# One of eight weight blocks of each expert is multiplied whole, in fp32

## The chip, the core and the metric

The kernel runs on one core of a Trainium2 chip. The metric is the device time in microseconds, the median of several runs. TensorE multiplies, VectorE and ScalarE work on rows of 128 partitions, GpSimd and SyncE mostly issue DMAs. A core has 16 DMA engines that share the transfers of all queues.

## What is computed

A graph layer on 384 tokens of 1024 features, in fp32: a normalisation, a graph attention with 16 heads, a linear attention block with a small feed-forward part, the sum of these with the input, a second normalisation, and last a mixture of eight experts. Only the experts are touched by the change:

```python
logits = t @ switch_w + switch_b
route_prob = softmax(logits)
routes = argmax(route_prob)
for e in range(8):
    h = gelu(t @ w1[e] + b1[e])      # w1[e]: 1024 x 512
    y = h @ w2[e] + b2[e]            # w2[e]: 512 x 1024
    out = where(routes == e, y, out)
out = out * max(route_prob)
```

## The kernel before

**Precision.** A product in fp32 is made of fp32r products. Each weight block (128 partitions x 1024, 512 KB) is copied by ScalarE to fp32r, its high part (L763 for the experts, L591 before them), and VectorE subtracts that from the raw block and gets the low part (L912, called from `prep_x`, L1218). In the expert stage the tokens' high and low parts stand side by side in one stationary operand (64 tokens each), so a block is multiplied by four fp32r products of 128 x 512: two halves, high and low part of the weights. The rows of the two token parts are added afterwards.

**The blocks.** An expert has eight blocks: four of w1 (up) and four of w2 (down). They come in the order up(0), up(1), down(0), up(2), down(1) and so on to up(7), down(6), down(7), and are numbered by q; from Q_WO on block q lies in ring slot (q - Q_WO) mod 8. Slots 0 to 3 are `raw` with splits in `wsp`, slots 4 to 7 `raw_x` with splits in two buffers named `big`. So the down blocks of the first seven experts lie in slots 0 to 3, the up blocks in 4 to 7, and the last expert's down blocks in 4 to 7.

**Loads.** SyncE (SP) issues all loads in order of q. Before load q it waits until VectorE has split block q - 8 (`w_lo`, L402). Behind the preloaded ring this is a loop with registers over experts (L409).

**TensorE.** Before the stage it gathers the tokens of each expert, beside the first up product. Then for e = 0 to 6: up(e+1) with L1788 and the bias L1796, down(e) with L1827 and the bias L1833, hidden(e+1) with L1811, which turns and folds the up result of fp32 by four fp32 products of 64 columns. Then down(7). A product waits for the splits of its block (`open_quarter`). down(e) waits for `ht_lo`, the low part of its hidden values.

**ScalarE**, for each e: three copies of blocks, the copy of the up result (L826), three copies, the low rows of y (L844), gelu (L834), the hidden values' high part (L836), two copies. The last block copied ahead of L844 is the second down block of expert e+1.

**VectorE**, for each e: six splits, the sum of y (L1414), the hidden values' low part (L912, tile `big<-work,big`), two splits.

**GpSimd** writes y of each expert to memory (L562, 256 KB), and after the last one gathers the rows of y per token (L573). VectorE adds them (L1478), and SyncE writes the output.

Of the kernel before, what the change touches and what calls it, by code (L numbers as in the profile page):

```python
# [20 lines left out]
F32 = mybir.dt.float32  # L21
# [51 lines left out]

WO_ORDER = ((0, 0), (0, 1), (0, 2), (0, 3), (1, 0), (1, 1), (1, 2), (1, 3))

class Tally:
# [36 lines left out]
def graph_layer(nc, x, rowb, cols, consts, later, src_rows, dst_rows, src_cols, dst_cols, type_cols,  # L115
                type_weights, w_stream, w_experts, switch_w, b12, out):
    with ExitStack() as ctx:
# [3 lines left out]
        def sem(name):  # L121
            return ctx.enter_context(nc.semaphore(name))
# [119 lines left out]
        piece_done, codes_done = sem("piece_done"), sem("codes_done")  # L242
        raw_in = [sem(f"raw_in{n}") for n in range(XRING)]
        w_hi, w_lo = sem("w_hi"), sem("w_lo")
        w_started = sem("w_started")
        acc_ready, acc_hi, acc_free = sem("acc_ready"), sem("acc_hi"), sem("acc_free")
        elu_parts, elu_hi = sem("elu_parts"), sem("elu_hi")
        elu_lo = sem("elu_lo")
# [43 lines left out]
        def raw_slot(k):  # L292

            if k < RING:
                return raw[:, k, :]
            return raw_x[:, k - RING, :]
# [48 lines left out]
        @block.sync  # L345
        def _(sp):
            for t in range(NT):
                sp.dma_start(tok[:, t, :], x[t * P:(t + 1) * P, :]).then_inc(x_in[t], 16)
            sp.dma_start(cst[:], consts).then_inc(const_in, 16)
            sp.dma_start(bias[:], cols).then_inc(const_in, 16)  # L350

            def load(row, slot, split):

                if split is not None:
                    sp.wait_ge(w_lo, split)
                sp.dma_start(raw[:, slot, :], w_stream[bass.ds(row, P), :]).then_inc(raw_in[slot], 16)

            def load_piece(first, buf, read):

                for k, r in enumerate((src_rows, dst_rows)):  # L360
                    if read is not None:
                        sp.wait_ge(codes_done, read)
                    sp.dma_start(edge_rows[buf][:, k, :],
                                 r[bass.ds(first, N)].partition_broadcast(P)).then_inc(piece_in[buf], 16)

            for q in range(RING):
                load(q * P, q, None)
            for j in range(2):
                load_piece(j * N, j, None)  # L370
            with sp.Fori(0, (Q_MV - RING) // RING) as i:
                for j in range(RING):
                    row = sp.snap(i * (RING * P) + (RING + j) * P)
                    load(row, j, i * RING + (j + 1))
                    if j % 2 == 0:
                        first = sp.snap(i * (2 * N) + (2 + j // 2) * N)
                        load_piece(first, j // 2, i * 2 + (j // 2 + 1))
            for q in range(Q_MV, Q_GQ + RING):
                load(q * P, q % RING, q - RING + 1)
                if q % 2 == 0 or q >= Q_GQ:  # L380
                    n = (q - Q_MV) // 2 + 8 if q < Q_GQ else q - Q_GQ + 12
                    load_piece(n * N, n % 2, n - 1)
            assert n == PIECES - 1
            with sp.Fori(0, (Q_PAIR0 - Q_GQ) // RING - 1) as i:
                for j in range(RING):
                    row = sp.snap(i * (RING * P) + (Q_GQ + RING + j) * P)
                    load(row, j, i * RING + (Q_GQ + j + 1))
            for q in range(Q_PAIR0, Q_PAIR):
                load(q * P, slot_of(q), q - RING + 1)
            with sp.Fori(0, PAIRS - 1) as i:  # L390
                for j in range(3):
                    row = sp.snap(i * (3 * P) + (Q_PAIR + j) * P)
                    load(row, 1 + j, i * 3 + (Q_PAIR + j - 2))
            for q in range(Q_WO, Q_WO + RING):
                load(q * P, slot_of(q), q - RING + 1)
            sp.wait_ge(w_started, Q_WO - 1)
            for q in range(Q_WO + RING, Q_MOE):
                sp.dma_start(raw_slot(slot_of(q)), w_stream[q * P:(q + 1) * P, :]).then_inc(raw_in[slot_of(q)], 16)

            def load_expert(row, k, split):  # L400

                sp.wait_ge(w_lo, split)  # L402
                sp.dma_start(raw_slot(k), w_experts[bass.ds(row, P), :]).then_inc(raw_in[k], 16)

            for j in range(RING):
                load_expert(j * P, j, Q_MOE + j - XRING + 1)

            with sp.Fori(0, EXPERTS - 1) as i:  # L409
                for k in range(XRING):  # L410
                    first = QE + k if k < RING else k
                    row = sp.snap(i * (QE * P) + first * P)
                    load_expert(row, (RING + k) % XRING, i * XRING + (Q_MOE + RING + k - XRING + 1))
            q = Q_MOE + QE * EXPERTS - RING
            for j in range(RING):
                k = slot_of(q + j)
                load_expert(((EXPERTS - 1) * QE + RING + j) * P, k, q + j - XRING + 1)

            sp.wait_ge(route_done, 1)  # L420
            over = sp.value_load(rowi[0:1, OVER:OVER + 1], min_val=0, max_val=OVER)
            with sp.If(over > 0):
                q += RING
                for o in range(OVER):
                    r = sp.value_load(rowi[0:1, o:o + 1], min_val=0, max_val=(EXPERTS - 1) * QE * P)
                    for j in range(QE):
                        row = sp.snap(r + j * P)
                        load_expert(row, slot_of(q), q - XRING + 1)
                        q += 1

            for t in range(NT):
                sp.wait_ge(sum_done, t + 1)
                sp.dma_start(out[t * P:(t + 1) * P, :], tok[:, t, :]).then_inc(out_done, 16)
            sp.wait_ge(out_done, 16 * NT)
# [144 lines left out]
        def _(act):  # L579
# [178 lines left out]
            def prep_x(started=None):  # L758

                slot = slot_of(q_no.n)  # L760
                act.wait_ge(raw_in[slot], used[slot].add(16))
                act.wait_ge(w_started, q_no.value - (XRING - 2) if started is None else started)
                nc.scalar.activation(split_of(slot, 0), raw_slot(slot), ACT.Copy).then_inc(w_hi, 1)  # L763
                q_no.add()
# [135 lines left out]
        def _(dve):  # L900
# [316 lines left out]

            def prep_x():  # L1218
                slot = slot_of(q_no.n)
                dve.wait_ge(w_hi, q_no.add())  # L1220
                lo(split_of(slot, 1), raw_slot(slot), split_of(slot, 0)).then_inc(w_lo, 1)

            def projected(h, t):
# [259 lines left out]
        def _(pe):  # L1483
# [295 lines left out]

            u_no, ht_no, y_no = Tally(), Tally(), Tally()  # L1780

            def up_block(s, e, base, j):

                open_quarter()
                for kk in range(2):
                    k = 2 * j + kk
                    for a in range(2):
                        ins = nc.tensor.matmul(ps[:, e % 2, :], slot_x(k, s),  # L1788
                                               split_of(base + j, a)[:, kk * HALF:(kk + 1) * HALF],
                                               start=(k == 0 and a == 0), stop=False)  # L1790
                        if kk == 0 and a == 0:
                            ins.then_inc(w_started, 1)
# [22 lines left out]
            def down(s, e, base):  # L1815

                pe.wait_ge(ht_lo, ht_no.add())
                if y_no.n > 1:
                    pe.wait_ge(y_sum, y_no.n - 1)
                y_no.add()  # L1820
                for j in range(4):
                    open_quarter()
                    bank = 4 + 2 * (e % 2) + j // 2
                    for kk in range(2):
                        k = 2 * (j % 2) + kk
                        for a in range(2):
                            ins = nc.tensor.matmul(ps[:, bank, :], htk[:, e % 2, k, :],  # L1827
                                                   split_of(base + j, a)[:, kk * HALF:(kk + 1) * HALF],
                                                   start=(k == 0 and a == 0), stop=False)
                            if kk == 0 and a == 0:  # L1830
                                ins.then_inc(w_started, 1)
                    if j % 2:
                        ins = nc.tensor.matmul(ps[:, bank, :], slot_hot(s),  # L1833
                                               b12r[:, F + (j // 2) * HALF:F + (j // 2 + 1) * HALF],
                                               start=False, stop=True)
                        if j == 1 and s == EXPERTS - 1:
                            ins.then_inc(y_half, 1)
                ins.then_inc(y_ready, 1)
# [119 lines left out]
```

## Time and profile before

| | |
|---|---|
| median of 3 runs | 637.99 us (637.88 to 639.61) |
| profiled execution | 641.52 us |
| its span, first to last instruction | 639.8 us, mean granted clock 0.964 |
| TensorE matmul, weight load | 569.8 us (89%), 519.7 us (81%) |
| VectorE | 458.3 us (72%) |
| ScalarE | 318.3 us (50%) |
| GpSimd | 177.2 us (28%) |
| DMA | 102.69 MB, mean 161 GB/s |

The shares are means over the whole span. The expert stage begins near 521 us with the gathers and ends with the last output near 640 us. From 540 to 622 us the experts' products run, and the experts' weights (64 blocks, 32 MB) come mostly in this time.

### The profile page before, as it was taken

What the parts mean: (1) busy time and instruction counts of PE and PEld (TensorE: products, weight loads), DVE (VectorE), ACT (ScalarE), POOL (GpSimd) and SP (SyncE); (2) the same over time, 40 slices, a digit from 0 to 9 for tenths busy, and PEclk for the clock granted to TensorE, in tenths of its full rate; (3) what the DMA queues carried; (4) which work ended last, traced back from release to release, by engine and by line L of the source; (5) the groups of instructions that cost most, each with busy time, mean ns of one, the idle gap of its engine ahead of it and who ended that gap; (6) DMA issues with size and microseconds to landing.
All of it is one profiled execution on the core that took longest, in us unless ns stands there. A gap on an engine that the chain in (4) does not pass through costs nothing.

```text
span 639.8 us, 9211 instructions
## 1 busy us (share of the span) xinstructions
PE 569.8 (89%) x3090; PEld 519.7 (81%) x3090; DVE 458.3 (72%) x807; ACT 318.3 (50%) x475; POOL 177.2 (28%) x167
## 2 busy tenths in 40 slices
PE   3699999999999999999999998999898769888970
PEld 2699997888999999999889888899786657766750
DVE  6678887885455444735679899787879655999972
ACT  3445553320333333534366655675653345998960
POOL 5556765856399000710001022100001100000001
PEclk9889999999999999999999999999899959999986
DMA  8356558450533433395322443422662212999936
GB/s 298 134 189 181 171 155 245 115 130 1 183 120 129 164 125 122 107 277 141 96 81 83 105 98 99 105 98 69 228 198 84 80 34 89 330 413 411 412 109 211
DMA packets 33043, 102.69 MB, mean 161 GB/s; under 512 B 5392, under 2 KB 9552, under 8 KB 33008
## 3 DMA queue, kind: packets, MB, share of 16 engines
q1 hardware_dynamic: 27792, 90.02, 41.8%
q0 software_dynamic: 4912, 11.46, 6.8%
q10 hardware_dynamic: 304, 0.79, 0.4%
q8 instruction: 18, 0.29, 0.2%
q14 instruction: 17, 0.14, 0.1%
HBM read 96.65 MB, written 5.60 MB: 160 GB/s over the span
## 4 chain that ended last, share of the span: by engine, by line
PE 53%; DVE 27%; ACT 8%; DMA 6%; issue 5%; POOL 1%; DVEq 0%; ACTq 0%; SPq 0%; POOLq 0%
PE ps L1506 31%; DVE wsp L912 7%; DVE big L912 4%; PE ps L1520 4%; DMA raw<-in_w_experts 3%; PE ps L1685 3%; PE ps L1576 2%; ACT work L712 2%; PE ps L1639 2%; PE ps L1775 2%; PE ps L1614 2%; ACT wsp L591 2%; DVE work L984 2%; DVE pt L912 2%; PE ps L1827 1%
## 5 line engine op out<-in xcount | busy, mean ns | idle before, releaser
L1506 PE MATMUL ps<-big,wsp 128*128 128x384 f32 x1680 | 304.2, 339 | 9.2 <-DVE wsp L912 6.6
L1506 PEld LDWEIGHTS ps<-big,wsp 128*128 128x128 f32 x1680 | 294.4, 190 | 14.0 <-DVE wsp L912 6.4
L912 DVE TENSOR_TENSOR wsp<-raw,wsp 128x1024 fp32r<-128x1024 f32 x117 | 149.9, 1292 | 29.4 <-ACT wsp L591 23.3
L591 ACT ACTIVATE wsp<-raw 128x1024 fp32r<-128x1024 f32 x83 | 87.2, 1053 | 33.5 <-PE ps L1520 12.9
L509 POOL DMA_INDIRECT edge_table<-ef,eidx x48 | 57.4, 1195 | 31.9 <-DMA edge_table<-ef,eidx 19.1
L465 POOL TENSOR_SCALAR rs<-mv 128x1 f32<-128x1 f32 x12 | 9.3, 779 | 199.5 <-DVE mv L1232 102.3
L598 ACT ACTIVATE big<-ps,bias 128x384 f32 x24 | 14.0, 583 | 83.0 <-PE ps L1506 83.0
L923 DVE SCALAR_TENSOR_TENSOR big<-ps,bias,big 128x384 f32 x24 | 14.8, 618 | 51.7 <-ACT big L598 49.7
L912 DVE TENSOR_TENSOR big<-raw_x,big 128x1024 fp32r<-128x1024 f32 x36 | 42.0, 1214 | 0.3 <-ACT big L763 0.3
L763 ACT ACTIVATE wsp<-raw 128x1024 fp32r<-128x1024 f32 x34 | 34.5, 1049 | 7.0 <-DMA raw<-in_w_experts 4.3
L1827 PE MATMUL ps<-wsp,big 128*128 128x512 f32 x112 | 28.8, 399 | 9.6 <-DVE big L912 9.6
L763 ACT ACTIVATE big<-raw_x 128x1024 fp32r<-128x1024 f32 x36 | 36.0, 1046 | 0.1
L712 ACT ACTIVATE work<-work,snm 128x384 f32<-128x384 f32 x48 | 28.9, 604 | 12.7 <-DVE snm L1132 12.7
L1827 PEld LDWEIGHTS ps<-wsp,big 128*128 128x128 f32 x112 | 20.5, 188 | 16.8 <-DVE big L912 12.6
L1520 PE MATMUL ps<-wsp,big 128*128 128x512 f32 x144 | 33.1, 390 | 0.3 <-DVE wsp L912 0.3
L562 POOL DMA_DIRECT2D slot_y<-maskb x7 | 3.8, 545 | 103.3 <-DVE maskb L1414 103.3
L1520 PEld LDWEIGHTS ps<-wsp,big 128*128 128x128 f32 x144 | 26.9, 188 | 6.3 <-DVE wsp L912 0.8
L984 DVE SCALAR_TENSOR_TENSOR work<-codes,ef,maskb 128x384 f32<-128x384 int32 (+2 forms) x48 | 21.8, 502 | 7.3 <-POOL codes L494 7.3
L1639 PE MATMUL ps<-pt,vp 128*128 128x384 f32 x96 | 20.4, 347 | 5.6 <-DVE pt L912 5.4
L1128 DVE CUSTOM_DVE_ANT_0 work<-ps,maskb 128x384 f32<-128x384 f32 x48 | 24.1, 565 | 0.9 <-issue 0.9
L1639 PEld LDWEIGHTS ps<-pt,vp 128*128 128x128 f32 x96 | 16.4, 188 | 8.9 <-issue 8.4
L728 ACT ACTIVATE low_rows<-ps 64x384 f32<-64x384 f32 x16 | 7.8, 489 | 31.5 <-PE ps L1639 31.4
(245 smaller groups left out, 847.5 us busy)
## 6 DMA issues: line engine op xcount, KB each, us to landing
raw<-in_w_stream SPq DMA_DIRECT2D x85, 512.0 KB, 3.5
raw<-in_w_experts SPq DMA_DIRECT2D x32, 512.0 KB, 6.5
raw_x<-in_w_experts SPq DMA_DIRECT2D x32, 512.0 KB, 6.8
rowbuf<-in_rowb POOLq DMA_DIRECT2D x6, 512.0 KB, 6.8
raw_x<-in_w_stream SPq DMA_DIRECT2D x4, 512.0 KB, 6.5
slot_y<-maskb POOLq DMA_DIRECT2D x7, 256.0 KB, 5.6
tok<-in_x SPq DMA_DIRECT2D x3, 512.0 KB, 4.4
edges_a<-in_src_rows SPq DMA_DIRECT2D x8, 192.0 KB
```

The lines of the kernel that those rows point to most:

```text
L509: pool.indirect_dma_start(out=table, out_offset=bass.IndirectOffsetOnAxis(ap=eidx[:, c:c + 1], axis=0), in_=ef[:, 3, c:c + 1], in_offset=N ...
L591: nc.scalar.activation(wsp[:, 0, slot, :], raw[:, slot, :], ACT.Copy).then_inc(w_hi, 1)
L712: nc.scalar.activation(probs[:, s, t, :], probs[:, s, t, :], ACT.Exp, bias=snm[:, s, t:t + 1], scale=DH ** -0.5, accum_out=ssum[:, s, t:t ...
L763: nc.scalar.activation(split_of(slot, 0), raw_slot(slot), ACT.Copy).then_inc(w_hi, 1)
L912: return nc.vector.tensor_tensor(dst, value, hi.bitcast(F32), ALU.subtract)
L984: ins = nc.vector.scalar_tensor_tensor(out=into[k], in0=codes[buf][:, k * P:N], scalar=ef[:, 0, bass.ds(c + k, 1)], in1=maskb[:, k, k * P: ...
L1128: ins = nc.vector.tensor_tensor_reduce(out=probs[:, s, t, :], in0=ps[:, 2 + 3 * s + t, 0:N], in1=maskb[:, t, :], scale=1.0, scalar=3.0 * N ...
L1506: ins = nc.tensor.matmul(ps[:, bank, 0:N], wsp[:, a, slot, k * P:(k + 1) * P], moving[:, b, k, :], start=(k == 0 and n == 0), stop=(k == K ...
L1520: ins = nc.tensor.matmul(ps[:, banks + t, :], stationary[:, b, k, t * P:(t + 1) * P], wsp[:, a, slot, kk * HALF:(kk + 1) * HALF], start=(k ...
L1639: ins = nc.tensor.matmul(ps[:, bank, 0:N], vp[:, mt, s, :], pt[:, b, mt, :], start=(mt == 0 and b == 0), stop=(mt == NT - 1 and b == 1))
L1685: ins = nc.tensor.matmul(ps[:, 2 + 3 * h + t, :], feat[0][:, b, k, t * P:(t + 1) * P], split_of(slot_of(Q_WO + h * RING + j), a)[:, kk * H ...
L1827: ins = nc.tensor.matmul(ps[:, bank, :], htk[:, e % 2, k, :], split_of(base + j, a)[:, kk * HALF:(kk + 1) * HALF], start=(k == 0 and a == ...
```

## The change

In each expert one down block is not split: the fourth of w2, in ring slot 3, for the last expert in slot 7. ScalarE and VectorE skip it. TensorE waits for its landing alone and multiplies the raw block, as fp32, by the hidden values read as fp32: two products in place of four. The next load into that ring slot waits for TensorE's last product of the block (`whole_done`), not for a split. SyncE's loop over experts becomes straight code, and the counts of splits that engines wait for leave the whole blocks out.

```diff
+WHOLE = frozenset([Q_MOE + QE * e + RING + 7 for e in range(EXPERTS - 1)] + [Q_MOE + QE * EXPERTS - 1])
+
+def split_count(q):
+    return q + 1 - sum(p <= q for p in WHOLE)
+
+def whole_count(q):
+    return sum(p <= q for p in WHOLE)
+
+def loads_of_slot(q):
+    return sum(slot_of(p) == slot_of(q) for p in range(q + 1))
...
-            def load_expert(row, k, split):
-                sp.wait_ge(w_lo, split)
-                sp.dma_start(raw_slot(k), w_experts[bass.ds(row, P), :]).then_inc(raw_in[k], 16)
+            def load_expert(row, q):
+                p = q - XRING
+                if p in WHOLE:
+                    sp.wait_ge(whole_done, whole_count(p))
+                else:
+                    sp.wait_ge(w_lo, split_count(p))
+                sp.dma_start(raw_slot(slot_of(q)), w_experts[bass.ds(row, P), :]).then_inc(raw_in[slot_of(q)], 16)
...
-            with sp.Fori(0, EXPERTS - 1) as i:
+            q = Q_MOE + RING
+            for e in range(EXPERTS - 1):
                 for k in range(XRING):
-                    first = QE + k if k < RING else k
-                    row = sp.snap(i * (QE * P) + first * P)
-                    load_expert(row, (RING + k) % XRING, i * XRING + (Q_MOE + RING + k - XRING + 1))
+                    load_expert((e * QE + (QE + k if k < RING else k)) * P, q + k)
+                q += XRING
...
             def prep_x(started=None):
                 slot = slot_of(q_no.n)
+                if q_no.n in WHOLE:
+                    used[slot].add(16)
+                    q_no.add()
+                    return
...
             def prep_x():
                 slot = slot_of(q_no.n)
-                dve.wait_ge(w_hi, q_no.add())
+                q_no.add()
+                if q_no.n - 1 in WHOLE:
+                    return
+                dve.wait_ge(w_hi, split_count(q_no.n - 1))
...
+            def open_block():
+                q = q_no.n
+                q_no.add()
+                if q in WHOLE:
+                    pe.wait_ge(raw_in[slot_of(q)], 16 * loads_of_slot(q))
+                else:
+                    pe.wait_ge(w_lo, split_count(q))
+                return q
...
-                        for a in range(2):
-                            ins = nc.tensor.matmul(ps[:, bank, :], htk[:, e % 2, k, :],
-                                                   split_of(base + j, a)[:, kk * HALF:(kk + 1) * HALF],
-                                                   start=(k == 0 and a == 0), stop=False)
+                        part = slice(kk * HALF, (kk + 1) * HALF)
+                        for a in range(1 if q in WHOLE else 2):
+                            if q in WHOLE:
+                                ins = nc.tensor.matmul(ps[:, bank, :], htk[:, e % 2, k, :].bitcast(F32),
+                                                       raw_slot(slot_of(q))[:, part], start=(k == 0), stop=False)
+                            else:
+                                ins = nc.tensor.matmul(ps[:, bank, :], htk[:, e % 2, k, :],
+                                                       split_of(base + j, a)[:, part],
+                                                       start=(k == 0 and a == 0), stop=False)
                             if kk == 0 and a == 0:
                                 ins.then_inc(w_started, 1)
+                    if q in WHOLE:
+                        ins.then_inc(whole_done, 1)
```

## Rows read from the trace of the kernel before

**Rows 1.** Stretches: us, length, busy us (count) per engine, clock, DMA share, GB/s.
```profile
552.00:564.00 12.00, 10.59 (x50) 8.19 (x48) 12.00 (x13) 11.38 (x16) 0.64 (x1) 1.00 1.02 405
588.00:600.00 12.00, 10.64 (x50) 8.27 (x49) 11.83 (x12) 11.31 (x14) 0.52 (x1) 1.00 1.03 412
```
**Rows 2.** Chain that ended last: start us, us, what.
```profile
567.49 4.54 DVE big L912 x4
...
574.48 9.23 DMA raw<-in_w_experts
```
**Rows 3.** Timeline, one expert: start, us, engine, line, tiles, count [idle before, releaser].
```profile
587.56 2.12 PE L1827 MATMUL ps<-wsp,big 128*128 128x512 f32 x8 [2.54 <-DVE big L912]
...
589.75 1.98 PE L1827 MATMUL ps<-wsp,big 128*128 128x512 f32 x8
...
598.36 0.50 PE L1827 MATMUL ps<-wsp,big 128*128 128x512 f32 x1 [1.34 <-DVE big L912]
...
589.95 4.62 DVE L912 TENSOR_TENSOR big<-raw_x,big 128x1024 fp32r<-128x1024 f32 x4
...
596.77 1.21 DVE L1414 TENSOR_TENSOR maskb<-ps,row_buf 64x1024 f32<-64x1024 f32 x1
597.90 0.41 DVE L912 TENSOR_TENSOR big<-work,big 128x256 fp32r<-128x256 f32 x1
```
**Rows 4.** Timeline of ScalarE: copies that waited for a load.
```profile
560.63 1.06 ACT L763 ACTIVATE wsp<-raw 128x1024 fp32r<-128x1024 f32 x1 [0.48 <-DMA raw<-in_w_experts]
...
594.53 1.06 ACT L763 ACTIVATE wsp<-raw 128x1024 fp32r<-128x1024 f32 x1 [0.19 <-DMA raw<-in_w_experts]
...
605.36 1.06 ACT L763 ACTIVATE wsp<-raw 128x1024 fp32r<-128x1024 f32 x1 [0.19 <-DMA raw<-in_w_experts]
```
**Rows 5.** Timeline of TensorE: starts of the first and the last two down products.
```profile
543.58 2.11 PE L1827 MATMUL ps<-wsp,big 128*128 128x512 f32 x8 [0.37 <-DVE big L912]
...
609.18 2.11 PE L1827 MATMUL ps<-wsp,big 128*128 128x512 f32 x8 [1.35 <-DVE big L912]
...
616.27 2.94 PE L1827 MATMUL ps<-big 128*128 128x512 f32 x8 [1.85 <-DVE big L912]
```
**Rows 6.** Records by line: ns min/median/max. L1571, L1788 are fp32r; L1714, L1811 fp32.
```profile
L1788 PE MATMUL ps<-big x84: 387/393/478, 538.2 to 606.3; 128*128 128x512 f32 x84
...
L1571 PE MATMUL ps<-ones_r,pt x18: 166/250/271, 141.7 to 153.5; 128*128 128x2 f32 x18
...
L1714 PE MATMUL ps<-swt,maskb x16: 170/256/256, 505.9 to 507.5; 128*128 128x8 f32 x16
...
L1811 PE MATMUL ps<-diag,work x64: 217/275/323, 540.1 to 614.1; 128*128 128x64 f32 x64
```
**Rows 7.** Timeline of SP's queue; last, landing of loads into `raw` from 540 us.
```profile
546.57 0.33 SPq L403 DMA_DIRECT2D raw<-in_w_experts  x1
547.73 3.72 SPq L403 DMA_DIRECT2D raw_x<-in_w_experts  x4
...
DMA to landing us min/median/max: 3.4/6.7/8.9
```
**Rows 8.** Short stretches at the start of the stage.
```profile
544.00:545.00 1.00, 1.00 (x6) 0.82 (x5) 0.96 (x1) 1.00 (x3) 0.00 (x0) 1.00 0.96 332
546.00:547.00 1.00, 1.00 (x6) 0.83 (x5) 1.00 (x2) 1.00 (x2) 0.00 (x0) 1.00 0.65 119
549.00:550.00 1.00, 1.00 (x7) 0.90 (x7) 1.00 (x2) 1.00 (x2) 0.00 (x0) 1.00 1.01 311
551.00:556.00 5.00, 3.65 (x16) 2.70 (x15) 5.00 (x6) 4.92 (x8) 0.64 (x1) 1.00 0.99 373
558.00:559.00 1.00, 1.00 (x7) 0.81 (x6) 1.00 (x2) 1.00 (x2) 0.00 (x0) 1.00 1.05 430
```
**Rows 9.** Short stretches of the last down product; the clock is the third number from the end.
```profile
618.00:619.00 1.00, 1.00 (x3) 0.73 (x3) 0.83 (x1) 0.00 (x0) 0.00 (x0) 0.50 0.36 78
620.00:621.00 1.00, 1.00 (x5) 0.77 (x4) 0.57 (x1) 0.33 (x1) 0.00 (x0) 0.65 0.08 16
```

More of the change, by code:

```diff
@@ L244, in graph_layer @@
         w_hi, w_lo = sem("w_hi"), sem("w_lo")
-        w_started = sem("w_started")
+        w_started, whole_done = sem("w_started"), sem("whole_done")
         acc_ready, acc_hi, acc_free = sem("acc_ready"), sem("acc_hi"), sem("acc_free")
@@ L398, in _ @@
                 sp.dma_start(raw_slot(slot_of(q)), w_stream[q * P:(q + 1) * P, :]).then_inc(raw_in[slot_of(q)], 16)
-            def load_expert(row, k, split):
-                sp.wait_ge(w_lo, split)
-                sp.dma_start(raw_slot(k), w_experts[bass.ds(row, P), :]).then_inc(raw_in[k], 16)
+            def load_expert(row, q):
[5 more added lines that the diff above has]
+                sp.dma_start(raw_slot(slot_of(q)), w_experts[bass.ds(row, P), :]).then_inc(raw_in[slot_of(q)], 16)
             for j in range(RING):
-                load_expert(j * P, j, Q_MOE + j - XRING + 1)
-            with sp.Fori(0, EXPERTS - 1) as i:
+                load_expert(j * P, Q_MOE + j)
+            q = Q_MOE + RING
+            for e in range(EXPERTS - 1):
                 for k in range(XRING):
-                    first = QE + k if k < RING else k
-                    row = sp.snap(i * (QE * P) + first * P)
-                    load_expert(row, (RING + k) % XRING, i * XRING + (Q_MOE + RING + k - XRING + 1))
-            q = Q_MOE + QE * EXPERTS - RING
+                    load_expert((e * QE + (QE + k if k < RING else k)) * P, q + k)
+                q += XRING
             for j in range(RING):
-                k = slot_of(q + j)
-                load_expert(((EXPERTS - 1) * QE + RING + j) * P, k, q + j - XRING + 1)
+                load_expert(((EXPERTS - 1) * QE + RING + j) * P, q + j)
             sp.wait_ge(route_done, 1)
@@ L427, in _ @@
                         row = sp.snap(r + j * P)
-                        load_expert(row, slot_of(q), q - XRING + 1)
+                        load_expert(row, q)
                         q += 1
@@ L1780, in _ @@
             u_no, ht_no, y_no = Tally(), Tally(), Tally()
+            def open_block():
[6 more added lines that the diff above has]
+                return q
             def up_block(s, e, base, j):
-                open_quarter()
+                open_block()
                 for kk in range(2):
@@ L1821, in down @@
                 for j in range(4):
-                    open_quarter()
+                    q = open_block()
                     bank = 4 + 2 * (e % 2) + j // 2
```

## The prediction

> **What bounds the kernel now.** The change touches nothing before the expert stage, so I read first the stretches of that stage, then the chain of work that ended last, then one expert in order of time. From 552 us two resources are full at once: VectorE is busy 12.00 of 12.00 us and still 11.83 of 12 from 588 us, and the DMA engines show a share of 1.02 to 1.03 at 405 to 412 GB/s [rows 1]. The chain says which of them ends last: up to 574 us it runs through VectorE's subtractions (one piece of four splits is shown), and from 574.48 us it crosses a load of 9.23 us [rows 2], and a second such load behind it. Three experts at VectorE's pace, the rest at the pace of the transfers.
>
> One expert in order of time [rows 3]: VectorE takes 4.62 us for four splits (1.155 each) and has eight: 9.2, plus the sum of y (1.13 to the next start) and the hidden split (about 0.3): 10.6 us. TensorE's down product starts at 587.56, the next at 598.36: 10.8 us, of which it idles 1.34 before the start. Its own work is therefore 9.46 us. The transfers: eight loads of 0.524 MB and 0.262 MB of y written back are 4.456 MB; at 412 GB/s that is 10.8 us. So per expert: transfers 10.8, VectorE 10.6, TensorE 9.5.
>
> What starts each down product is fixed by the code: ScalarE splits the second down block of the next expert, copies the low rows of y, then gelu, and VectorE follows. From the landing of that block (594.53, where ScalarE had waited for the DMA) to the down product (598.36) are 3.8 us; the same from 605.36 to 609.18 [rows 3, 4, 5]. I call it the gate block. The first that ScalarE waits for lands at 560.63, the last that counts at 605.36: 44.7 us for four experts [rows 4].
>
> **What the change removes.** Eight ScalarE copies and eight VectorE subtractions, one pair per expert: 1.155 us of VectorE, which falls to 9.4 us per expert. For experts at the transfers' pace this is worth nothing on the path; for the first three it would be worth up to 10.6 minus the next limit.
>
> **What it adds on TensorE.** Four fp32r products of 512 columns go and two fp32 ones come. Eight fp32r products run in 1.98 us [rows 3]; with 0.387 for one alone [rows 6] the spacing is (1.98 - 0.387)/7 = 0.2275, a block 0.91 us. The trace has no fp32 product of 512 columns. 
>
> TensorE becomes 9.5 + 0.8 = 10.3 us per expert, below 10.8. So in the middle of the stage the 0.8 is covered by TensorE's idle 1.34 us, and would cost itself if the transfers were faster. At the end it is bare twice: the y of the seventh expert is waited for by ScalarE and through it by the eighth down product (start 609.18 to 616.27), and the eighth down product ends the stage [rows 5]. 2 x 0.8 = **+1.6 us**.
>
> **What it moves: the wait on SP.** A load into the ring slot of a whole block waits for TensorE to finish that block, not for VectorE's split. Every load is on SP's queue in order, so behind this wait stand the four up blocks and the first down blocks of later experts. In the trace of before the first such load goes out at 546.57 [rows 7]. After: the down product starts at 543.58, and its last block begins 2 + 0.23 + 4 x 0.2275 = 3.1 us later, plus 1.7: 548.4. So 1.9 us later. The next three (547.73 on, 1.155 apart) were free by VectorE, now a split earlier, and leave at SP's own pace of 0.33 to 0.4 us; by the fourth the delay is gone. In a later expert it is the same: at 587.56 the split of that block ended at 590.0, TensorE would end it at 592.4, so 2.4 us later.
>
> Does a late load cost anything when the queue is deep? A load alone lands in 3.4 us, of which about 1.3 is its bytes, so its data start some 2 us after its issue; the median is 6.7 [rows 7], so some five are under way. At 592.4 there are the gate block (landing 594.53), one more, and the end of another; the new bytes start at 594.5. The queue thins to two but doesn't empty. What thin queues move: 332 GB/s with the stage's first two loads out (544 us), 119 with the queue nearly run out (546), 311 with about three (549), 430 with many (558) [rows 8]. Some 2.5 us at 330 in place of 412 lose 0.5 us. So **an expert costs 10.8 + 0.5 = 11.3 us**, between 10.8 (no loss) and 12.2 (2 us at 119). Four experts: 45.2 against 44.7, **+0.5 us** (-1.5 to +4.1). Before's own 44.7 is more than 4 x 10.8 = 43.2 since, as its queue grew, later loads shared the engines with the gate block; a thinner queue takes some of that back, and the low bound counts all of it.
>
> At the start of the stage the queue is thin already. A hole of 1.9 us there loses about 300 x 1.9 = 0.57 MB, 1.4 us at 412. The loads that then come in a burst would fill 551 to 556 us, which before ran at 373 [rows 8]: 5 x 39 = 0.2 MB, 0.5 us, come back. **+0.9 us** (0 to 1.9).
>
> VectorE's gain in the first three experts is lost in this: the pace of the transfers takes over earlier. SP's loop with registers becomes straight code; its register work (about 0.1 us per load) lies in its waits: 0. The whole block waits for its landing alone, and it lands 2 us before TensorE wants it: 0.
>
> **The sum.** 1.6 + 0.5 + 0.9 = +3.0 us. The profiled execution has a span of 639.8 and took 641.52 in all (1.7 around the span), 3.5 above the median of the runs. Its span would be 642.8, its time 644.5; the median 637.99 + 3.0 = **641.0**.
>
> The clock: in the last down product, which started after TensorE had idled 1.85 us, the granted clock was 0.50 (1.2 GHz) from 618 to 619 and 0.65 from 620 to 621, so full again from 620.7 [rows 5, 9]. Its first eight products took 2.94 us for 2.0, so it fell at about 617.3: 3.4 us at half speed cost 1.7 us. I leave it as it is. If it doesn't fall, 1.7 us less; if the last whole block lies in it, 0.85 x 2 = 1.7 more at most.
>
> **Rivals.** (1) VectorE was the bound, and taking work off it speeds the stage up: faster. From the first down product at 543.58 to the seventh are six experts, at TensorE's new 10.3 us: 605.4 in place of 609.18, -3.8, plus 1.6: -2.2, so 635.8. For it speaks that VectorE is full and that the chain runs through it until 574 us. It decides from 4.456 MB in 10.3 us, 433 GB/s; the highest microsecond read shows 430 and the long stretches 404 to 412, which speaks against. The Trainium skill ("DMA: Bandwidth & Descriptors", Where 436 GB/s comes from) puts the ports' ceiling at 435 GB/s; by it this rival would need all of it, on this trace's 412 it falls. Chance 0.10.
> (2) The transfers end when they did: hole and thin queue are made good by the smaller skew (0.9 - 1.5 or thereabouts), and what remains is the tail. Between -0.6 + 1.6 = +1.0 and +1.6, or about 0 if fp32 costs as little as the low bound (the change then brings nothing anywhere): 638 to 639.8. Chance 0.28.
> (3) The queue starves: the late load empties the ring each time, 12.2 us per expert. 0.9 + 4.1 + 1.6 = +6.6: 644.6. It decides if what is out at TensorE's signal ends before the new bytes start. Two loads against 2 us speak against it, the 119 GB/s for it. Chance 0.12.
>
> **How the numbers follow.** My forecast has 0.50. A measurement of this kernel can tell 0.3%, 1.9 us, from no change. Faster 0.10 (rival 1), same 0.28 (rival 2), slower 0.62 (forecast and rival 3). The range goes from 637.2 (rival 2 with some of the clock given back) to 644.7 (rival 3), and leaves out rival 1 and what lies beyond rival 3.
>
> **What would show it.** Right: whole blocks of about 1.7 us with four records of twice fp32r's spacing; the load behind the first whole block issued near 548.4; dips of the rate to about 330 GB/s once per expert; down products 11 us apart with ScalarE waiting for the DMA before them; VectorE idle about 1 us per expert; the seventh down product near 610.6. Wrong: down products 10.3 us apart (rival 1); the last loads landing no later than 611 (rival 2); stretches near 119 GB/s (rival 3); a block near 0.9 us; a clock that stays at 1.0 in the last product.

## The result, and the profile after

The changed kernel took 643.85 us, the median of 12 runs (640.47 to 646.40), beside 638.18 of 12 runs of the kernel before. The medians lie 5.7 us apart. The ratio on record, which is not the quotient of the medians, is 1.0079 with a 95% interval from 1.0056 to 1.0101: 5.0 us slower, 3.6 to 6.4. Every ratio below is of this kind, and the us beside it are worked out from it. One of the 12 runs of before took 1139.26 us, and the narrow interval shows that it is not in the ratio. A second timing gave 1.0061 (1.0030 to 1.0092), 3.9 us, with medians of 642.76 and 639.25. Forecast were +3.0 us, 641.0, and a range of 637.2 to 644.7: both medians lie within the range, the first near its upper end. The profiled execution took 644.38 us with a span of 642.6 (forecast: 644.5 and 642.8).

Stretches of the expert stage after, with the columns of [rows 1]:

```profile
552.00:564.00 12.00, 11.95 (x53) 8.99 (x53) 10.44 (x10) 9.53 (x12) 0.64 (x1) 1.00 1.01 383
564.00:576.00 12.00, 10.52 (x46) 7.50 (x44) 10.72 (x11) 10.29 (x13) 0.54 (x1) 1.00 1.03 409
576.00:588.00 12.00, 9.98 (x43) 7.39 (x43) 10.52 (x10) 10.07 (x13) 0.52 (x1) 1.00 1.02 404
588.00:600.00 12.00, 9.99 (x43) 7.39 (x43) 10.57 (x11) 10.16 (x12) 0.55 (x2) 1.00 1.01 400
```

VectorE, full in [rows 1], has 10.4 to 10.7 of 12 us: the relief is there, and the kernel is no faster for it. The DMA engines are as full as they were and move less, 383 to 409 GB/s in place of 405 to 412. The chain that ended last shows it more plainly than any share:

```profile
563.23 8.90 DMA raw<-in_w_experts
...
574.50 8.62 DMA raw<-in_w_experts
...
585.49 9.48 DMA raw<-in_w_experts
...
597.33 8.79 DMA raw<-in_w_experts
```

In [rows 2] VectorE's splits carried it until 574 us; now it crosses one load in every expert from the third on. The whole block by line (records as in [rows 6]), and TensorE's timeline around the last two down products:

```profile
L1865 PE MATMUL ps<-raw,big x28: 590/592/592, 547.6 to 615.5; 128*128 128x512 f32 x28
```
```profile
611.12 2.11 PE L1868 MATMUL ps<-wsp,big 128*128 128x512 f32 x8 [1.05 <-DVE big L935]
613.07 0.40 PE L1876 MATMUL ps<-big,qp 128*128 128x512 f32 x1
613.30 1.07 PE L1868 MATMUL ps<-wsp,big 128*128 128x512 f32 x4
614.21 1.88 PE L1865 MATMUL ps<-raw,big 128*128 128x512 f32 x4
615.53 0.79 PE L1876 MATMUL ps<-big,qp 128*128 128x512 f32 x1
616.16 1.00 PE L1847 MATMUL ps<-diag,work 128*128 128x64 f32 x8
619.01 2.14 PE L1868 MATMUL ps<-big 128*128 128x512 f32 x8 [1.85 <-DVE big L935]
```

Four records in 1.88 us, 0.592 for one: a spacing of (1.88 - 0.592)/3 = 0.43 us, 1.72 us for the block against 0.91. From the seventh down product (611.12) to the eighth (619.01) are 7.89 us; in [rows 5] they are 7.09 apart. That is the bare 0.8 us.

The hold on the ring slot, from SP's queue and short stretches at the start of the stage:

```profile
549.51 0.33 SPq L425 DMA_DIRECT2D raw<-in_w_experts  x1
549.89 1.38 SPq L425 DMA_DIRECT2D raw_x<-in_w_experts  x3
```
```profile
548.00:549.00 1.00, 1.00 (x5) 0.48 (x3) 1.00 (x2) 1.00 (x2) 0.00 (x0) 1.00 0.89 324
549.00:550.00 1.00, 1.00 (x8) 0.72 (x7) 1.00 (x2) 1.00 (x2) 0.00 (x0) 1.00 0.30 107
550.00:551.00 1.00, 1.00 (x8) 0.91 (x8) 1.00 (x2) 1.00 (x2) 0.00 (x0) 1.00 0.56 147
551.00:556.00 5.00, 4.95 (x22) 3.77 (x21) 5.00 (x6) 3.97 (x6) 0.64 (x1) 1.00 1.01 377
```

Over the stage SP's queue waits six times for the whole block (L1865), 19.7 us in all and up to 3.6 at once. That is how long the queue stood, not what it cost:

```profile
SPq L425 <- PE ps L1865: 19.7, 6, 3.6
```

The first down product started at 544.53 here. The load behind the first whole block went out 4.98 us after that, in [rows 5, 7] 2.99 us after: 2.0 us late. Two microseconds at 107 and 147 GB/s are the hole; in a later expert the rate dips once, as at 602 us to 311. Before has a thin spot there too (119 at 546 us, [rows 8]), so the loss is read over 15 us from the first down product, first in before, then in after:

```profile
543.58:558.58 15.00, 13.31 (x60) 10.47 (x61) 14.54 (x14) 14.92 (x19) 0.64 (x1) 1.00 0.91 323
544.53:559.53 15.00, 14.95 (x61) 10.86 (x62) 13.81 (x13) 13.37 (x17) 0.64 (x1) 1.00 0.87 301
```

That is 4.84 MB against 4.51; the other profiles of the two kernels have 5.03 and 4.80 against 4.33 and 4.41. The mean loss is 0.47 MB, 1.1 us at 412 GB/s. And where the weights stop coming, again first in before, then in after:

```profile
610.00:611.00 1.00, 1.00 (x6) 0.82 (x5) 1.00 (x2) 1.00 (x3) 0.00 (x0) 1.00 1.06 328
611.00:612.00 1.00, 1.00 (x6) 0.83 (x5) 0.98 (x2) 1.00 (x2) 0.00 (x0) 1.00 0.43 131
613.00:614.00 1.00, 1.00 (x7) 0.79 (x6) 1.00 (x2) 0.53 (x1) 0.00 (x0) 1.00 0.95 361
614.00:615.00 1.00, 1.00 (x4) 0.55 (x3) 0.98 (x1) 0.00 (x0) 0.00 (x0) 1.00 0.18 66
```

The rate falls near 611 us in before and near 613.5 in after, whose first down product is 0.95 us later: counted from there, the transfers end almost 2 us later.

**How far one profile carries.** When the stage begins varies from execution to execution, whichever kernel it is: the first down product stands between 540.0 and 544.5 us in the 14 profiles taken. So I compare times within the stage. Each is a difference of rows of TensorE's timeline; the last column ends at the start of VectorE's third sum of y, the last arithmetic of the kernel.

| kernel | six experts (1st to 7th down product) | 7th to 8th | 8th to the last sum |
|---|---|---|---|
| before, three profiles | 65.60, 64.98, 65.26 | 7.09, 7.07, 7.09 | 19.05, 19.01, 19.26 |
| after, three profiles | 66.59, 65.56, 66.50 | 7.89, 7.90, 7.88 | 19.23, 19.94, 19.59 |
| straight | 64.36 | 7.11 | 16.92 |
| wait_only | 65.72 | 7.09 | 19.69 |
| no_tail | 66.08 | 7.08 | 18.85 |
| copy_fp32b | 64.73 | 7.92 | 19.54 |
| half_product | 65.48 | 7.07 | 18.72 |
| copy_no_tail | 64.51 | 7.07 | 17.38 |
| light_after | 60.25 | 8.65 | 19.45 |
| light_straight | 63.90 | 7.11 | 18.91 |

By the means, after loses 0.9 us over six experts, 0.8 between the last two, 0.5 behind: 2.2 us. The runs lose more, and a part of the rest is the clock. Over all runs a mean granted clock lower by 0.001 goes with 0.5 us more, and a straight line through time and clock leaves a spread of 1.1 us. Read at the same clock, the runs of after stand 3.9 and 3.7 us above those of before, each within 0.7. I give this reading for each experiment beside its ratio. It is a fit, and part of the clock may itself be an effect of the change. It sets every kernel against all runs of before, on four chips; the runs of before that stood beside the first timing have no clock on record. Against the runs of before on its own chip the second timing of after stands at 3.1 and not 3.7, and the other kernels move by 0.2 or less. The difference of two kernels is known within 0.9 by the pooled fit.

### The profile page after: what moved, and what is told of

The parts are those of the page before. It is cut to its first block, busy times and chain, and to the rows that moved or that the text cites. A ratio compares the mean times of both kernels' runs of the same rounds, so it can differ in the third digit from the quotient of the medians.

```text
span 642.6 us, 9004 instructions
## 1 busy us (share of the span) xinstructions
PE 574.3 (89%) x3090; PEld 519.7 (81%) x3090; DVE 454.1 (71%) x799; ACT 312.7 (49%) x467; POOL 177.8 (28%) x167
## 3 DMA queue, kind: packets, MB, share of 16 engines
q0 software_dynamic: 4912, 11.46, 6.5%
## 4 chain that ended last, share of the span: by engine, by line
PE 53%; DVE 23%; DMA 9%; ACT 8%; issue 4%; POOL 2%; ACTq 0%; DVEq 0%; SPq 0%; POOLq 0%
PE ps L1532 31%; DVE wsp L935 6%; DMA raw<-in_w_experts 6%; PE ps L1546 4%; PE ps L1711 2%; PE ps L1602 2%; ACT work L731 2%; PE ps L1665 2%; DVE big L935 2%; PE ps L1801 2%; ACT wsp L610 2%; PE ps L1640 2%; DVE work L1007 2%; DVE pt L935 2%; PE ps L1868 1%
## 5 line engine op out<-in xcount | busy, mean ns | idle before, releaser
L935 DVE TENSOR_TENSOR wsp<-raw,wsp 128x1024 fp32r<-128x1024 f32 x110 | 144.6, 1319 | 32.2 <-ACT wsp L610 23.3
L610 ACT ACTIVATE wsp<-raw 128x1024 fp32r<-128x1024 f32 x83 | 87.2, 1052 | 34.1 <-PE ps L1546 12.9
L1546 PE MATMUL ps<-wsp,big 128*128 128x512 f32 x144 | 33.2, 390 | 0.3 <-DVE wsp L935 0.3
L1546 PEld LDWEIGHTS ps<-wsp,big 128*128 128x128 f32 x144 | 26.9, 188 | 6.3 <-DVE wsp L935 0.8
L786 ACT ACTIVATE wsp<-raw 128x1024 fp32r<-128x1024 f32 x27 | 27.9, 1051 | 7.6 <-DMA raw<-in_w_experts 4.4
L1868 PE MATMUL ps<-wsp,big 128*128 128x512 f32 x84 | 22.3, 401 | 7.0 <-DVE big L935 7.0
L1868 PEld LDWEIGHTS ps<-wsp,big 128*128 128x128 f32 x84 | 15.2, 188 | 13.0 <-DVE big L935 10.0
```

What stands on the lines that cost most here:

```text
L610: nc.scalar.activation(wsp[:, 0, slot, :], raw[:, slot, :], ACT.Copy).then_inc(w_hi, 1)
L935: return nc.vector.tensor_tensor(dst, value, hi.bitcast(F32), ALU.subtract)
L1546: ins = nc.tensor.matmul(ps[:, banks + t, :], stationary[:, b, k, t * P:(t + 1) * P], wsp[:, a, slot, kk * HALF:(kk + 1) * HALF], start=(k ...
```

## The experiments

In the diffs `MARKED` is the set of blocks that the change calls `WHOLE`.

**Straight code alone (straight).**

```diff
-WHOLE = frozenset([Q_MOE + QE * e + RING + 7 for e in range(EXPERTS - 1)] + [Q_MOE + QE * EXPERTS - 1])
+WHOLE = frozenset()
```

> No block is whole; all that is left of the change is that SP's loop over the experts is straight code. My theory (the cost is the ring slot's hold and the fp32 products): 0, within 0.6 us of before. Rival (the straight code on SP costs by itself, through its own fetches or later issues): a part of the +5.0 us, 1 us or more.

Measured: 639.26, ratio 1.0008 (0.9980 to 1.0036), at equal clock +0.8 within 0.7. The straight code alone does not cost 5 us; whether it costs half a microsecond or one these runs can't tell.

**The wait alone (wait_only).**

```diff
+                if p in MARKED:
+                    sp.wait_ge(whole_done, whole_count(p))
...
+                    if q in MARKED:
+                        ins.then_inc(whole_done, 1)
```

> All blocks are split and multiplied in fp32r as before, but the load into the marked block's slot waits for TensorE to finish that block. So it has the hold and neither the fp32 product nor the relief of VectorE. My theory: the first such load goes out 1.1 us late instead of 1.9, the queue thins for less long: +0.5 to +1.2 us. Rival (the hold costs nothing, fp32 is the whole price): 0.

Measured: 642.72, ratio 1.0054 (1.0025 to 1.0082), +3.4 us; at equal clock +2.5, against the straight code +1.7 within 0.9. More than I expected, and not 0: the hold costs by itself, with all splits and products as before. Its load went out 4.2 us after the first down product (543.46), 1.2 later than in before:

```profile
547.67 0.33 SPq L426 DMA_DIRECT2D raw<-in_w_experts  x1
548.04 3.15 SPq L426 DMA_DIRECT2D raw_x<-in_w_experts  x4
```

**No whole block in the last two experts (no_tail).**

```diff
+WHOLE = frozenset([Q_MOE + QE * e + RING + 7 for e in range(EXPERTS - 2)])
```

> The changed kernel with the last two experts' blocks split again; the first six are whole. My theory: the two bare fp32 products go, -1.6 us against the changed kernel, +3.4 against before. Rival (all of the cost is in the transfers): +5 as the changed kernel. The last down product starts 7.1 us behind the one before it, not 7.9.

Measured: 642.73, ratio 1.0070 (1.0039 to 1.0101), +4.5; at equal clock +2.5, so 1.2 to 1.4 below after (each within 0.9; 0.6 when the second timing is set against its own chip). The last two down products are 7.08 us apart. The raw ratios of this kernel and of after overlap, so they alone would not have told 1.6 us from 0; the profile's 0.8 us shows the first half, and the second is read from the last product below.

**Whole and fp32, but without the hold (copy_fp32b).** ScalarE copies the block, as fp32, to a place that is idle in the stage, and the slot is free after that.

```diff
+                    nc.scalar.activation(copied[:], raw_slot(slot), ACT.Copy).then_inc(whole_in, 1)
...
-                    sp.wait_ge(whole_done, whole_count(p))
+                    sp.wait_ge(whole_in, whole_count(p))
...
-                                                       raw_slot(slot_of(q))[:, part], start=(k == 0), stop=False)
+                                                       copied[:, part], start=(k == 0), stop=False)
```

> The block is multiplied whole in fp32 as in the changed kernel, but from a copy that ScalarE makes into 4 KB per partition that are idle in this stage, so the ring slot is free after that copy, some 4 us before TensorE is done. VectorE still saves its split. My theory: the hold goes, so first to seventh down product take what they take without it (64.4 us in the kernel with straight code alone, 66.6 in the changed kernel); what stays is 2 x 0.8 us at the end: +1.6 us against before. Rival (VectorE was the bound): down products 10.3 us apart, 62 us for the six, and about 0 or less. Rival (the hold costs nothing): as the changed kernel, +5.

Measured: 640.89, ratio 1.0034 (1.0006 to 1.0062), +2.2; at equal clock +1.8. This is the clearest run for the two rivals. If the hold cost nothing it would stand where after stands, and it is 2 us below within 0.9. It does a little more than take the hold away: the load behind the first whole block went out 2.2 us after the down product, in before 3.0. If VectorE were the bound its six experts would take 62 us, and they took 64.73:

```profile
541.59 2.11 PE L1873 MATMUL ps<-wsp,big 128*128 128x512 f32 x8 [0.37 <-DVE big L940]
552.36 2.14 PE L1873 MATMUL ps<-wsp,big 128*128 128x512 f32 x8 [0.81 <-DVE big L940]
562.35 2.11 PE L1873 MATMUL ps<-wsp,big 128*128 128x512 f32 x8
572.64 2.12 PE L1873 MATMUL ps<-wsp,big 128*128 128x512 f32 x8 [0.33 <-DVE big L940]
584.69 2.12 PE L1873 MATMUL ps<-wsp,big 128*128 128x512 f32 x8 [2.06 <-DVE big L940]
595.50 2.11 PE L1873 MATMUL ps<-wsp,big 128*128 128x512 f32 x8 [0.81 <-DVE big L940]
606.32 2.14 PE L1873 MATMUL ps<-wsp,big 128*128 128x512 f32 x8 [0.85 <-DVE big L940]
```

Two experts run at TensorE's pace, 9.99 and 10.29 us, the next takes 12.05, and then they come every 10.8 us. What was gained by going ahead was given back when the bytes ran out: ScalarE waited for a load there.

```profile
579.58 1.06 ACT L791 ACTIVATE wsp<-raw 128x1024 fp32r<-128x1024 f32 x1 [1.63 <-DMA raw<-in_w_experts]
```

**Half of the fp32 product (half_product).** Each of the block's two products covers 256 of its 512 columns.

```diff
-                                ins = nc.tensor.matmul(ps[:, bank, :], htk[:, e % 2, k, :].bitcast(F32),
-                                                       raw_slot(slot_of(q))[:, part], start=(k == 0), stop=False)
+                                ins = nc.tensor.matmul(ps[:, bank, 0:HALF // 2], htk[:, e % 2, k, :].bitcast(F32),
+                                                       raw_slot(slot_of(q))[:, kk * HALF:kk * HALF + HALF // 2],
+                                                       start=(k == 0), stop=False)
```

> The changed kernel with each whole block's two fp32 products over 256 of 512 columns; half of the block's result is left out, the output is another. The block costs TensorE 0.86 us as in before, hold and relief of VectorE stay, the hold is 0.85 us shorter. My theory: 2 x 0.8 us less at the end and up to 1 us less from the shorter hold: +2.4 to +3.4 against before; seventh to eighth down product 7.1 us apart. Rival (all lies in the hold and the transfers): +5.

Measured: 641.24, ratio 1.0049 (1.0021 to 1.0076), +3.1, within what was expected; at equal clock only +1.0, 2.6 to 2.9 below after. The seventh and eighth down products are 7.07 us apart. The price of fp32 is real, and it lengthens the hold as well: the load behind the first whole block went out at 548.05, 4.1 us after the down product at 543.91, not 5.0.

**Fewer bytes, with the change (light_after) and without it (light_straight).** The 24 up blocks loaded in the stage come by half.

```diff
+                if slot_of(q) >= RING and Q_MOE + XRING <= q < Q_MOE + QE * EXPERTS - RING:
+                    sp.dma_start(raw_slot(slot_of(q))[:, 0:HALF], w_experts[bass.ds(row, P), 0:HALF])\
+                        .then_inc(raw_in[slot_of(q)], 16)
```

> The changed kernel, but of the 24 up blocks loaded in the stage only the first 512 of 1024 columns come (what stays in the ring is used for the rest, the output is another). An expert moves 3.41 MB in place of 4.46, 8.3 us at 412 GB/s. My theory (bytes bind): down products at TensorE's 10.0 to 10.3 us instead of 11.3, the six in 61 us, some -3 us against before. Rival (the late signal and the landing time bind, whatever the bytes): they stay at 11 us or more.

> The kernel with straight code alone and nothing whole, with the same halved up loads (another output). My theory: VectorE binds at once, 10.55 us per expert through all seven, the six in 63.5 us: -1 us against before, and now slower than the changed kernel with the same loads, as the relief of VectorE has found its use. Rival (TensorE or something else binds): another pace.

Measured: with the whole blocks 637.42, ratio 0.9982 (0.9956 to 1.0009), without them 638.39, ratio 0.9998 (0.9971 to 1.0025). The intervals of these two overlap; at equal clock the first stands at -1.7 and the second at 0.0, 1.7 apart within 1.0. Six experts take 60.25 us with the change (10.0 each) and 63.90 without (10.55 each from the second on). One stretch of each, first with the whole blocks, then without:

```profile
576.00:588.00 12.00, 12.00 (x54) 8.70 (x52) 11.81 (x12) 11.34 (x14) 0.53 (x1) 1.00 0.98 350
```
```profile
576.00:588.00 12.00, 10.00 (x47) 8.07 (x48) 12.00 (x13) 11.69 (x15) 1.05 (x2) 1.00 0.92 319
```

With the bytes gone, TensorE is full in the first (12.00 of 12) and VectorE in the second. So the change is worth 3.6 us over these six experts where the transfers allow it, and the hold, which is still there, shows no cost while TensorE is full. In the real kernel the same relief meets 4.46 MB per expert. Between the seventh and the eighth down product the first of the two lost 0.76 us against after (8.65 to 7.89). There VectorE's sum of y, which the later steps follow, waited for the write of the y before it:

```profile
609.31 1.22 DVE L1445 TENSOR_TENSOR maskb<-ps,row_buf 64x1024 f32<-64x1024 f32 x1 [2.38 <-DMA slot_y<-maskb]
```

**The two kernels once more (before_b, before_c, after_b).**

> The kernel before once more, for a second profile of its expert stage. One theory: the first profile held one slow expert (11.74 us between down products 4 and 5, where the kernel with straight code alone had 10.55), so that its 65.6 us for six experts is high and 64.4 is usual. Other theory: straight code on SP gained those 1.2 us, and the kernel before stays at 65.6.

> As the run beside it, a third profile of the kernel before: 64.4 us for six experts by the one theory, 65.6 by the other.

> The changed kernel once more, for a second profile: 66.6 us for six experts, 7.9 us from the seventh down product to the eighth. If this differs by over 0.5 us, the loss in the stage varies from run to run.

The six experts of before took 64.98 and 65.26 us, between the two theories' numbers; the fifth down product came late again, 11.07 and 11.38 us behind the fourth. So the late expert of the first profile is no accident: VectorE's pace of 10.55 outruns the transfers for three experts, and then the down product has to wait for them, as the chain in [rows 2] does from 574.48 us. The one profile of straight has no such expert (10.55 there), and its 64.36 lies below all three of before; whether straight code helps there or that execution was a quick one stays open, as its runs are not faster. After's varied by 1.0 us from profile to profile.

**Neither hold nor tail (copy_no_tail).**

```diff
+WHOLE = frozenset([Q_MOE + QE * e + RING + 7 for e in range(EXPERTS - 2)])
```

on top of ScalarE's copy.

> Whole blocks for the first six experts alone, multiplied from ScalarE's copy. It has neither the hold nor a bare fp32 product. My theory: the bytes bind, so VectorE's relief is worth nothing and the time is that of before: 0, within 1 us, six experts in 64.4 us, seventh to eighth 7.1 us. Rival (VectorE's relief pays when nothing stands against it): -2 us, which would beat both kernels.

Measured: 638.22, ratio 0.9996 (0.9965 to 1.0027), at equal clock -0.4 within 0.7: the time of before. It frees VectorE of six splits and gains nothing that can be measured against before. Against straight, with which it shares the code on SP, it stands 1.2 us lower at equal clock within 0.9, with six experts in 64.51 us against 64.36; so a gain of a microsecond from the relief is not excluded.

**The second timing (after_c).**

> The changed kernel a third time, timed again beside the kernel before. What is open: the profiles' expert stages differ by less than the medians. One theory: the first ratio (1.0079) stands high by chance, and the change costs what its steps add up to, +2.5 to +4 us (1.004 to 1.006). Other theory: the loss of 5 us is real and again about 1.008, with a part in most executions that the profiled ones don't show. In the profile: six experts in 65.5 to 66.6 us, 7.9 us to the eighth down product.

Measured: 642.76, ratio 1.0061 (1.0030 to 1.0092), six experts in 66.50 us, 7.88 us to the eighth down product. It lies between the theories and excludes neither; the two intervals overlap from 1.0056 to 1.0092, so 3.6 to 5.9 us can hold for both.

## Why the prediction was right, and where its terms were off

The direction and the mechanism hold, and the time lies within its range, 2 us or more above the forecast by the first timing and about 1 by the second. That the profiled execution came within 0.2 us of its forecast (642.6 for 642.8) was in part luck: its first down product stood 0.95 us later than in before, where nothing was changed, and its last product kept the full clock, worth 1.6 us the other way (below). Point by point:

- **TensorE's price.** 1.7 us per block forecast, 1.72 measured; 2 x 0.8 at the end forecast, 0.80 measured between the seventh and eighth down products. The second 0.8 is blurred in the last column of the table (0.5 by its means) by GpSimd's gather and the writes, but shown before them, at the last row sum (the point on the clock): 0.8. By the runs: copy_fp32b, which has this price alone, stands at +1.8 at equal clock, and no_tail 1.2 to 1.4 below after. The Trainium skill's four passes ("FP8 and Floating Point Precision", TensorE Precision Notes) agree with 4 records at 0.43 us, twice fp32r's 0.2275 each.
- **The hold.** The late load was forecast 1.9 us late and was 2.0. Its price was forecast as 0.9 + 0.5 = 1.4 us. The runs say about 2: after stands 1.9 to 2.1 above copy_fp32b at equal clock, wait_only 1.7 above straight. Each is within 0.9, and against its own chip's before the second timing is only 1.1 above copy_fp32b, whose slot is also free earlier than before's. The profiles say 1.4 (65.72 against 64.36) and 1.5 (after's mean 66.22 against 64.73). So the hold costs 1 to 2 us; that 1.4 was too small is not shown. The bytes came out a little worse than forecast: at the start 0.57 - 0.2 = 0.37 MB net, measured 0.47. The transfers end almost 2 us later, but the seventh down product starts only 0.9 later. Its gate block comes some 5 us ahead of the last bytes (605.36 against 611 in before), and I read the difference as the smaller skew that rival 2 counted on: it took back about half. In the later experts the queue did stay filled, as forecast: the dips are to 311, not to 119.
- **VectorE's relief** was put at zero in the whole, right in its sum and wrong in its course. I had the transfers' pace "take over earlier". In fact the second down product came 10.01 us after the first in place of 11.15, and the third 11.46 after it in place of 10.54: 1.14 us gained, then 0.92 lost. First to third is 21.47, 21.88 and 21.87 us in after's profiles against 21.69, 21.70 and 21.70, so the opening cost 0.0 on average, not 0.9. Without the hold it is 20.76 and 20.75 (copy_fp32b, copy_no_tail): there the relief is worth 0.9 us, and the hold takes it away again.
- **Third to seventh down product**: 45.2 us forecast against 44.7 (my reading of the gate blocks). Measured 45.12, 43.68 and 44.63, against 43.91, 43.28 and 43.56: +0.9, not +0.5. The two errors nearly cancel over the six experts: +0.9 measured, +1.4 forecast.
- **Rival 1** (VectorE the bound) falls with this kernel's bytes and holds without them: light_after against light_straight shows its 10.0 us per expert, a little below the 10.3 I had put in. So the 9.46 us that I read as TensorE's own work was too much by some 0.3 us. **Rival 2** (the transfers end when they did; its upper end is 637.99 + 1.6 = 639.6, not 639.8) falls: they end almost 2 us later, and the hold costs by itself in wait_only. **Rival 3** (starvation, 12.2 us per expert) falls: single experts took up to 11.9 us, and the six 10.9 to 11.1 on average.
- **The clock** was left as it was in before. In the profiles it varies: it fell in the last down product in all three of before and in two of after, and stayed at 1.00 in the first profile of after, in straight and in copy_no_tail. Where it stayed, without a whole block, the last column of the table is 16.9 and 17.4 us; where it fell, 18.9 to 19.7. A closer reading ends at VectorE's last sum of y (L1422, after it L1448), ahead of the gather. From the start of the eighth down product it comes after 6.65 us in before, where the clock fell, and after 5.90 in the first profile of after, where it did not:

```profile
622.92 0.68 DVE L1422 TENSOR_TENSOR maskb<-ps,row_buf 64x512 f32<-64x512 f32 x1 [1.81 <-ACT row_buf L851]
```
```profile
624.91 0.68 DVE L1448 TENSOR_TENSOR maskb<-ps,row_buf 64x512 f32<-64x512 f32 x1 [2.05 <-ACT row_buf L874]
```

Over all profiles with a full last block or none, the four cases are: clock kept, nothing whole, 5.04 and 5.05; clock kept, whole, 5.90; clock fallen, nothing whole, 6.62 to 6.66; clock fallen, whole, 7.46 and 7.47. So the whole block costs 0.8 to 0.9 us at either clock, and the fall costs 1.6, where I had put 1.7. The prediction named a clock that stays at 1.00 as a sign of being wrong. It came once in after's three profiles, and in straight too; so it tells executions apart and not these kernels. One row of straight, where TensorE had idled 1.85 us just as in [rows 5]:

```profile
616.00:618.00 2.00, 2.00 (x10) 1.67 (x9) 1.31 (x2) 0.60 (x1) 0.00 (x0) 1.00 0.13 29
```

**What stays open.** The steps are 0.9, 0.8 and 0.8 us, 2.5 in all with the last product at the same clock (2.2 as the profiles stand). The runs say 3.7 to 3.9 at equal clock (3.1 for the second timing by its own chip), and the ratios 3.9 and 5.0. The three profiled executions of after have spans of 642.6, 639.7 and 640.2 us against 639.8, 636.9 and 640.3, 1.8 more on average; brought to one clock like the runs, they stand 3.0 above, and three against three is known within 1.8 only. So profiles and runs do not contradict each other, but no run settled where the part beyond 2.5 us lies. A part of the difference may be that all three profiles of before had the slow last product, which its median run need not have. Whether the change itself lowers the mean clock (0.9627 and 0.9646 on average, before 0.9653) stays open too.

## What to carry to other kernels

When two resources are full in the same stretch, taking work off one is worth nothing until the other has room; halving the loads of the up blocks in both kernels showed in one stretch which was which. A buffer that is read by a later engine is held longer, and everything behind its load on the queue waits as well: cost the hold apart from the work that is saved, and look for a copy that gives the buffer back early (here it took back a part of the loss, not all). A profile of one execution gives the steps and their places; the size of a half-percent effect needs many runs and the clock beside them.

## What was not expected of the hardware

A record of an fp32r product that follows the fp32 ones has 0.79 us in place of 0.40 (613.07 against 615.53 in the timeline above), and the next one starts 0.63 us after it in place of 0.23. The 0.4 us fit the end of the fp32 block's 1.72 us (614.21 + 1.72 = 615.93). I read it so that the last record's columns are still running when the bias product is shown to start; no run tests this.

The DMA share says less than it seems to. In before, some three loads under way showed a share of 1.01 and moved 311 GB/s [rows 8], where the long stretches show the same share at 412. A share near 1 does not say that the transfers run at their rate.
